# K's first set stored in two halves, warm-up matmuls ahead of it, the second set before head 0

## The chip, the cores and the metric

The kernel runs on one core of one Trainium2 chip. The metric is the device time of one launch in microseconds, median of three runs: 210.45 us before the change (210.29 to 210.97). The engines of the core are TensorE (PE, with its weight loads as PEld), VectorE (DVE), ScalarE (ACT), GpSimd (POOL) and SyncE (SP), which only issues transfers. They run their own programs and meet by semaphores.

## The reference

x has shape (128, 32, 512): batch, head, time. Stage one is a long convolution with a kernel K that is computed from small parameters, plus D times the input, masked by a length per batch; stage two is a linear layer with bias and a low-rank adapter chosen per batch row. Both add to x.

```
dtA = A * dt[:, None]                       # A = -exp(log_A_real) + 1j * A_imag
Ct  = Cc * (exp(dtA) - 1) / A
K   = 2 * einsum('hn,hnl->hl', Ct, exp(dtA[:, :, None] * arange(L))).real
y   = irfft(rfft(u, 2L) * rfft(K, 2L))[..., :L] + u * D[:, None]
x   = x + y * (arange(L) < length)
x   = x + (x @ base_weight.T + base_bias + (x @ A[id].T) @ B[id].T)
```

## The kernel before

**K.** The lag l is written as 32 a + c, so that exp(dtA l) is a product of two factors and K of one head is a small matrix product, 16 x 32, over 128 rows (64 states, real and imaginary part). VectorE makes dt, the angles and their fraction of a turn, ScalarE the magnitudes (one Exp per head, L504), the sines (L468) and th, POOL the division's parts (`sm`, `mm`, `rc`, `ez`; L353 to L376), and VectorE joins them into the coefficients `ct` (`coefficients`, L659 to L664). The heads are done in four sets of 8 (`GROUPS`). For a set VectorE runs `turns`, `phases`, `whole`, `fraction` (L684 to L698), then ScalarE the sine, then VectorE `multiply` and `scale` (L706 to L713), which write the factors `gg` and `ee`. TensorE's `group(k)` multiplies them into a PSUM bank `k_ps` (L913) and adds D to lag 0 by one more product with a unit row (L915).

**The store of K.** `group_store(k)` on ScalarE rounds the PSUM rows to the short float format (`k_hi`, L479), copies them to `k_sb` (L482), waits for VectorE's `k_low(k)`, the remainder (L670), and issues the store to the DRAM buffer `k_pad` on ScalarE's own DMA queue (L487). High and low parts lie beside each other.

**The convolution.** Head h's Toeplitz matrix is read from `k_pad` as a `strip` of 128 rows, each shifted by one lag (L263, 512 KB with both parts, six buffers). The input of a head, `z_all`, comes by pairs of heads (L240, 512 KB; eight pairs first, the others in between by the table `X_AT`). ScalarE rounds it into `xp` (L462), VectorE takes the remainder (L741). `head(h)` on TensorE does 12 matmuls per head into `z_ps` (L932), and VectorE writes the masked result over `z_all` (L747). A strip is issued when the head six before it is done. Set 0 and set 1 of K are made before head 0, sets 2 and 3 by TensorE after heads 7 and 14 (`K_AFTER`; their vector work is spread by `STEPS_AT`).

**The order on SP.** One program order sets all large transfers: parameters, eight x pairs, then, once set 0 of K is in DRAM (wait at L272), strips 0 to 31 with the later x pairs, the adapter tables A and B and the weights W in halves between them (`X_AT`, `A_AT`, `B_AT`, `W_AT`), x_tile 0 and 1, the two parts of the B table, the bias, x_tile 2 and 3 (L266), and then one tile in and one out per step.

**Warm-up.** `keep_warm(n)` issues n matmuls of 512 columns whose result is not used (L904): 15 between the products of sets 0 and 1, and 2 before head 0.

**Stage two.** 32 tiles of 128 rows: `x1_of` adds the convolution to x (L792), ScalarE rounds (L558), `x1_remainder` follows (L796), `tile_h` multiplies by the gathered A (L959), `h_masked` (L802 to L806), `h_rounded` (L570) and `h_remainder` (L811) prepare h, ScalarE and POOL gather the next A (L550, L412), `tile_base` is the weight product (L971), `tile_b` adds B (L997, L998).

## Time and profile before

| what | us |
|---|---|
| median of 3 runs | 210.45 |
| the profiled execution, its time | 210.57 |
| its span on the core | 208.5 |
| head 0 begins | 21.5 |
| stage two begins (first weight matmul) | 87.07 |
| TensorE busy | 190.8 (91%) |
| VectorE busy | 168.1 (81%) |

The span is what the instructions cover; about 2 us of the launch lie around it. The page divides the span into 40 slices and gives a digit of busy share for each, and the chain of work that ended last is followed back from the last instruction. Line numbers are those of the kernel before.

### The profile page before, as it was taken

Reading aid. Unit: us, or ns where it says so; the run is one execution under the profiler, and the core shown is the slowest. Engines: PE = TensorE matmul, PEld = TensorE weight load, DVE = VectorE, ACT = ScalarE, POOL = GpSimd, SP = SyncE. Lnnn points to the kernel's source line nnn. Section 1 sums busy time; section 2 is a strip of 40 time slices with the busy share of each in tenths; the row PEclk is TensorE's granted clock in tenths of the full one; section 3 lists DMA queues with packets and bytes.
Section 4 is the critical chain, followed back from the end, with each engine's and each line's share of the span. In section 5 each row is a group of like instructions: output and inputs, shape, how many; then the busy total and the mean of one; then the engine's idle time right before and its main releaser. Section 6 shows DMA issues by size and latency. Waiting matters only on the chain.

```text
span 208.5 us, 4394 instructions
## 1 busy us (share of the span) xinstructions
PE 190.8 (91%) x1063; PEld 166.4 (80%) x1063; DVE 168.1 (81%) x368; ACT 120.9 (58%) x354; POOL 90.3 (43%) x144
## 2 busy tenths in 40 slices
PE   0049999999999999899999999999999999999994
PEld 0037999999999899787888888888888888888883
DVE  3985598789799976877999978788888878888662
ACT  2798974343736446237767656657566565656530
POOL 4850000001356778085564645546455464545500
PEclk9999999999999999999999999999999999999999
DMA  5973999999999999983767666677776676765324
GB/s 141 400 310 105 377 410 409 409 413 406 412 411 407 409 407 422 339 262 105 257 238 247 217 207 228 214 201 224 213 222 204 216 229 201 218 200 186 103 101 151
DMA packets 21520, 56.46 MB, mean 271 GB/s; under 512 B 3266, under 2 KB 3970, under 8 KB 21250
## 3 DMA queue, kind: packets, MB, share of 16 engines
q1 hardware_dynamic: 18002, 47.55, 62.2%
q0 software_dynamic: 2560, 8.39, 13.3%
q10 hardware_dynamic: 944, 0.36, 0.7%
q8 instruction: 5, 0.08, 0.2%
q14 instruction: 9, 0.07, 0.1%
HBM read 45.64 MB, written 10.65 MB: 270 GB/s over the span
## 4 chain that ended last, share of the span: by engine, by line
PE 87%; DMA 6%; DVE 4%; POOL 1%; issue 1%; DVEq 0%
PE z_ps L932 26%; PE y_ps L971 20%; PE k_ps L971 20%; PE z_ps L959 7%; DMA strip<-k_pad 5%; PE y_ps L904 3%; PE y_ps L998 2%; PE y_ps L997 2%; PE k_ps L998 2%; PE k_ps L997 2%; PE k_ps L913 1%; DMA par<-params 1%; PE y_ps L1020 1%; PE k_ps L1020 1%; PE y_ps L981 1%
## 5 line engine op out<-in xcount | busy, mean ns | idle before, releaser
L932 PE MATMUL z_ps<-xp,strip 128*128 128x512 f32 (+3 forms) x384 | 63.4, 326 | 0.3 <-DMA strip<-k_pad 0.3
L932 PEld LDWEIGHTS z_ps<-xp,strip 128*128 128x128 f32 x384 | 59.3, 196 | 4.3 <-DMA strip<-k_pad 0.4
L417 POOL DMA_INDIRECT b_hl<-b_tab,b_idx x32 | 37.7, 1178 | 15.3 <-issue 8.5
L412 POOL CAST ag<-a_hl 128x128 fp32r x64 | 23.3, 367 | 41.0 <-PE z_ps L959 30.4
L971 PE MATMUL y_ps<-w_hi,xp 128*128 128x512 f32 x120 | 39.5, 390 | 0.0
L971 PE MATMUL k_ps<-w_hi,xp 128*128 128x512 f32 x120 | 39.5, 390 | 0.0
L550 ACT ACTIVATE ag<-a_hl 128x64 fp32r x128 | 25.6, 249 | 20.5 <-issue 20.3
L462 ACT ACTIVATE xp<-z_all 128x512 fp32r<-128x512 f32 x32 | 19.7, 627 | 19.7 <-PE z_ps L932 18.2
L741 DVE TENSOR_TENSOR xp<-z_all,xp 128x512 fp32r<-128x512 f32 x32 | 26.5, 827 | 5.3 <-ACT xp L462 5.2
L971 PEld LDWEIGHTS y_ps<-w_hi,xp 128*128 128x128 f32 x120 | 22.5, 188 | 4.3
L971 PEld LDWEIGHTS k_ps<-w_hi,xp 128*128 128x128 f32 x120 | 22.5, 188 | 4.2
L747 DVE TENSOR_TENSOR z_all<-z_ps,mask 128x512 f32<-128x512 f32 (+2 forms) x33 | 22.1, 669 | 4.2 <-PE z_ps L932 3.9
L570 ACT ACTIVATE h_hi<-h_m 64x128 fp32r<-64x128 f32 x64 | 19.5, 305 | 9.1 <-DVE h_m L806 7.0
L971 PE MATMUL y_ps<-w_lo,xp 128*128 128x512 f32 x60 | 23.4, 390 | 0.0
L971 PE MATMUL k_ps<-w_lo,xp 128*128 128x512 f32 x60 | 23.4, 390 | 0.0
L399 POOL TENSOR_TENSOR a_hl<-a_raw,a_hl 128x512 fp32r<-128x512 f32 x4 | 6.0, 1512 | 38.5 <-ACT a_hl L540 38.5
L558 ACT ACTIVATE xp<-x_t 128x512 fp32r<-128x512 f32 x30 | 19.0, 632 | 5.5 <-DVE x_t L792 4.8
L959 PEld LDWEIGHTS z_ps<-xp,ag 128*128 128x128 f32 x128 | 19.3, 188 | 3.4 <-issue 0.5
L792 DVE TENSOR_TENSOR x_t<-x_t,z_all 128x512 f32<-128x512 f32 x30 | 20.5, 684 | 0.6 <-DMA x_t<-x_tile 0.6
L796 DVE TENSOR_TENSOR xp<-x_t,xp 128x512 fp32r<-128x512 f32 x30 | 20.3, 677 | 0.7 <-ACT xp L558 0.7
L959 PE MATMUL z_ps<-xp,ag 128*128 128x256 f32 x128 | 20.2, 281 | 0.1
L563 ACT ACTIVATE h_b<-z_ps 64x256 f32<-64x256 f32 x32 | 12.1, 379 | 12.4 <-PE z_ps L959 12.4
(138 smaller groups left out, 239.4 us busy)
## 6 DMA issues: line engine op xcount, KB each, us to landing
strip<-k_pad SPq DMA_DIRECT2D x31, 512.0 KB, 7.9
z_all<-x_conv SPq DMA_DIRECT2D x16, 512.0 KB, 8.5
x_t<-x_tile SPq DMA_DIRECT2D x32, 256.0 KB, 2.8
out<-a_raw SPq DMA_DIRECT2D x31, 256.0 KB, 2.4
a_raw<-a_t SPq DMA_DIRECT2D x2, 512.0 KB, 8.3
x_t<-b_rows SPq DMA_DIRECT2D x2, 512.0 KB, 8.8
w_sb<-w_t SPq DMA_DIRECT2D x2, 512.0 KB, 10.0
b_tab<-b_hl SPq DMA_DIRECT2D x1, 1024.0 KB, 10.1
```

The lines of the kernel that those rows point to most:

```text
L412: last = g.tensor_copy(ag[:, s, :, :, q, :].rearrange("p c e r -> p e c r"), src)
L417: g.indirect_dma_start(out=b_hl[:, t % BS, :].bitcast(F32), out_offset=None, in_=b_tab, in_offset=bass.IndirectOffsetOnAxis(ap=b_idx[:, t: ...
L462: act.activation(xp[:, h % XS, :, 0, :], z_all[:, h, :, :], ACT.Copy).then_inc(xc_hi_done, 1)
L550: last = act.activation(ag[:, s, :, e, q, :], src[:, e, :, :], ACT.Copy)
L570: act.activation(h_hi[o:o + BR, b, :], h_m[:, b, :], ACT.Copy).then_inc(hhi_done, 1)
L741: V.tensor_tensor(xp[:, h % XS, :, 1, :], z_all[:, h, :, :], xp[:, h % XS, :, 0, :].bitcast(F32), ALU.subtract).then_inc(xc_lo_done, 1)
L747: V.tensor_tensor(z_all[:, h, :, b0:b1], in_chunks(z_ps[:, h % ZS, :])[:, :, b0:b1], mask[:, :, b0:b1], ALU.mult).then_inc(z_masked, 1)
L792: V.tensor_tensor(xt, xt, z_rows(t), ALU.add).then_inc(x1_done, 1)
L796: V.tensor_tensor(xp[:, s % XS, :, 1, :], in_chunks(x_t[:, s % XT, :]), xp[:, s % XS, :, 0, :].bitcast(F32), ALU.subtract).then_inc(xlo_do ...
L932: last = nc.tensor.matmul(z_ps[:, h % ZS, m * P:L], strip[:, h % SS, m * P:(m + 1) * P, t], xp[:, h % XS, 0:LC - m, e, :], start=(n == 0), ...
L959: last = nc.tensor.matmul(h_ps[:, s % TS, 0:2 * P], ag[:, s % TS, c, :, :, :].rearrange("p e b r -> p (e b r)"), xp[:, s % XS, c, :, :].re ...
L971: last = nc.tensor.matmul(y_bank(s), xp[:, s % XS, c, e, :], w[:, c, :], start=(n == 0), stop=False)
```

## The change

- `GROUPS` becomes five: set 0 is multiplied, rounded and stored as two groups of four heads, and `SETS` keeps the four sets of 8 for the sines. The two PSUM banks and buffers are used in turn (`KS` = 2), each with its own semaphore `k_stored[s]`.
- ScalarE rounds straight into `k_sb` (`rounded_rows`), so that the second copy is gone. It does so after 3, 2 and 3 of the second set's magnitudes.
- The first three stores are issued by SP (`store_k`), the first two before and after the last of the eight x pairs, the third at h = 6. The last two are issued by ScalarE as before.
- Strip 1 is loaded in halves as strip 0.
- TensorE issues 12 warm-up matmuls as soon as POOL has set a buffer to one, 5, 4, 4 and 5 after four events of the preparation, then groups 0 and 1, then 10, 3 and 5 more, and the product of the second set, all before head 0.
- For the sets 2 and 3 the D matmul is replaced by an addition by VectorE in PSUM (`k_first_lag`).
- On POOL the unit matrix is built later, two operations of `mm` come before the reciprocal's result, and two scalings go to ScalarE (L516 and L517 of the changed kernel). The factor 2 is in the table.
- One x pair and one half of W come one head later in SP's order.

```
-GROUPS = ((0, 8), (8, 16), (16, 24), (24, 32))
+SETS = ((0, 8), (8, 16), (16, 24), (24, 32))
+GROUPS = ((0, 4), (4, 8), (8, 16), (16, 24), (24, 32))
-X_AT = {7: 8, 10: 9, 13: 10, 15: 11, 18: 12, 20: 13, 22: 14, 24: 15}
+X_AT = {7: 8, 10: 9, 13: 10, 15: 11, 18: 12, 20: 13, 22: 14, 25: 15}
-A_AT, B_AT, W_AT = {9: 0, 12: 1}, {17: 0, 19: 1}, {24: 0, 26: 1}
+A_AT, B_AT, W_AT = {9: 0, 12: 1}, {17: 0, 19: 1}, {24: 0, 27: 1}
-K_AFTER = {2: 7, 3: 14}
-WARM_0, WARM_1 = 15, 2
+K_AFTER = {3: 7, 4: 14}
+WARM = (12, 5, 4, 4, 5)
+WARM_K = (10, 3, 5)
...
-            for n in range(2, PRE):
+            for n in range(2, PRE - 1):
                 load_pair(n)
+            for k in range(KS):
+                sp.wait_ge(k_lo_done, k + 1)
+                store_k(sp, k)
+                if k == 0:
+                    load_pair(PRE - 1)
...
+                if h == SS:
+                    sp.wait_ge(k_lo_done, BY_SP)
+                    store_k(sp, BY_SP - 1)
                 if h >= SS:
                     sp.wait_ge(conv_done, h + 1 - SS)
-                if h == 0:
-                    load_strip(h, 0, 0, L // 2, strip_begun)
-                    load_strip(h, 0, L // 2, L, strip_landed[0])
+                if h < 2:
+                    load_strip(h, h, 0, L // 2, strip_begun[h])
+                    load_strip(h, h, L // 2, L, strip_landed[h])
...
             g.memset(zero[:, :], 0.0).then_inc(zeroed, 1)
+            pool.wait_ge(zeroed, 1)
+            g.memset(xp[:, XS - 1, :, 0, :].bitcast(F32), 1.0).then_inc(warm_ready, 1)
...
+            link(g.tensor_tensor(mm[:, 1, 1, :], sm[:, 6, :], sm[:, 4, :], ALU.subtract))
+            link(g.tensor_tensor(mm[:, 1, 0, :], sm[:, 5, :], sm[:, 7, :], ALU.add))
             pool.wait_ge(th_ready, 1)
...
             g.tensor_tensor(ez[:, :], th_1[:, :], rr[:, 1, :], ALU.mult).then_inc(ez_ready, 1)
-            link(g.tensor_tensor(mm[:, 1, 1, :], sm[:, 6, :], sm[:, 4, :], ALU.subtract))
-            link(g.tensor_tensor(mm[:, 1, 0, :], sm[:, 5, :], sm[:, 7, :], ALU.add))
...
-            magnitudes(*GROUPS[1])
-            group_store(0)
-            group_sines(1)
+            magnitudes(8, 11)
+            rounded_rows(0)
+            magnitudes(11, 13)
+            rounded_rows(1)
+            magnitudes(13, 16)
+            set_sines(1)
             split_x(1)
-            magnitudes(16, 18)
-            group_store(1)
+            magnitudes(16, 17)
+            rounded_rows(2)
+            magnitudes(17, 19)
             split_x(2)
-            magnitudes(18, 24)
+            magnitudes(19, 24)
+            act.wait_ge(warmed, 1)
             split_x(3)
...
+            def k_first_lag(k):
+                (h0, h1), s = GROUPS[k], k % KS
+                dve.wait_ge(k_done, k + 1)
+                lag_0 = k_ps[0:1, s, 0:(h1 - h0) * NC:NC]
+                V.tensor_tensor(lag_0, lag_0, d_sb[:, h0:h1], ALU.add).then_inc(d_added, 1)
```

TensorE's program up to the first strip matmuls of head 0, before the change:

```order
L913 MATMUL k_ps<-ee,gg 16x32 [waits factors,zeroed,d_in]
L913 MATMUL k_ps<-ee,gg 16x32 x7
L915 MATMUL k_ps<-d_sb,row 16x8
L904 MATMUL y_ps<-xp 128x512 [waits xc_hi_done]
L904 MATMUL y_ps<-xp 128x512 x14
L913 MATMUL k_ps<-ee,gg 16x32 [waits factors]
L913 MATMUL k_ps<-ee,gg 16x32 x7
L915 MATMUL k_ps<-d_sb,row 16x8
L904 MATMUL y_ps<-xp 128x512 x2
L932 MATMUL z_ps<-xp,strip 128x512 [waits xc_lo_done,strip_begun]
```

And the same place of the changed kernel, from the warm-ups (L951) that wait for the angle on:

```order
L951 MATMUL y_ps<-xp 128x512 [waits sines_ready]
L951 MATMUL y_ps<-xp 128x512 x4
L962 MATMUL k_ps<-ee,gg 16x32 [waits factors,zeroed,d_in]
L962 MATMUL k_ps<-ee,gg 16x32 x3
...
L951 MATMUL y_ps<-xp 128x512 x10
L951 MATMUL y_ps<-xp 128x512 [waits reduced]
L951 MATMUL y_ps<-xp 128x512 x2
L951 MATMUL y_ps<-xp 128x512 [waits sines_ready]
L951 MATMUL y_ps<-xp 128x512 x4
L962 MATMUL k_ps<-ee,gg 16x32 [waits k_lo_done,factors]
L962 MATMUL k_ps<-ee,gg 16x32 x7
L967 MATMUL k_ps<-d_sb,row 16x8
```

Eighteen warm-ups now stand between `turn_ready` and the first product, where none stood, and the product of the second set comes directly before head 0.

SP's issues from the x pairs to strip 8, before the change:

```order
L240 DMA z_all<-x_conv 128x1024 x6
L263 DMA strip<-k_pad 128x512 [waits k_stored,pad_stored]
L263 DMA strip<-k_pad 128x512
L263 DMA strip<-k_pad 128x1024 x5
L283 DMA ids<-ids_all 128x160
L263 DMA strip<-k_pad 128x1024 [waits conv_done] x2
L240 DMA z_all<-x_conv 128x1024
L263 DMA strip<-k_pad 128x1024 [waits conv_done,k_stored]
```

And in the changed kernel:

```order
L250 DMA z_all<-x_conv 128x1024 x5
L230 DMA k_pad<-k_sb 16x4x64 [waits k_lo_done]
L250 DMA z_all<-x_conv 128x1024
L230 DMA k_pad<-k_sb 16x4x64 [waits k_lo_done]
L279 DMA strip<-k_pad 128x512 [waits k_stored0,pad_stored]
L279 DMA strip<-k_pad 128x512 x3
L279 DMA strip<-k_pad 128x1024 x2
L279 DMA strip<-k_pad 128x1024 [waits k_stored1]
L279 DMA strip<-k_pad 128x1024
L302 DMA ids<-ids_all 128x160
L230 DMA k_pad<-k_sb 16x8x64 [waits k_lo_done]
L279 DMA strip<-k_pad 128x1024 [waits conv_done] x2
```

Three stores of K have moved into SP's queue, two of them ahead of the first strip with one x pair between them, and the third behind strip 5 and the ids.

## Rows read from the trace of the kernel before

**Rows 1.** The page: DMA share in 40 slices, and the chain by engine.
```profile
DMA  5973999999999999983767666677776676765324
...
PE 87%; DMA 6%; DVE 4%; POOL 1%; issue 1%; DVEq 0%
```

**Rows 2.** The chain of waits to 60 us: start, duration, what.
```profile
13.44 1.01 PE k_ps L913 x16
14.45 0.15 PE k_ps L915 x2
...
21.51 15.60 PE z_ps L932 x96
```

**Rows 3.** Timeline of ACT from 10 to 16 us: start, duration, engine, line, operation.
```profile
10.25 0.63 ACT L468 ACTIVATE work<-work 128x512 f32<-128x512 f32 x1 [0.31 <-DVE work L698]
...
12.71 1.91 ACT L504 ACTIVATE mag<-tab,zr 128x48 f32<-128x48 f32 x8
14.64 0.37 ACT L479 ACTIVATE k_hi<-k_ps 16x256 fp32r<-16x256 f32 x1
...
15.65 0.33 ACTq L487 DMA_DIRECT2D k_pad<-k_sb  x1
```

**Rows 4.** Timeline of DVE from 7 to 16 us.
```profile
7.32 0.18 DVE L650 TENSOR_SCALAR cs_x<-an 128x32 f32<-128x32 f32 x1
...
11.29 0.29 DVE L662 TENSOR_TENSOR cs_m<-cs,mm 128x128 f32<-128x128 f32 x1 [0.60 <-POOL mm L376]
...
11.88 0.42 DVE L706 TENSOR_TENSOR work<-work,ct 128x256 f32<-128x256 f32 x1
...
15.14 0.41 DVE L670 TENSOR_TENSOR k_sb<-k_ps,k_hi 16x256 f32<-16x256 f32 x1
15.48 0.67 DVE L698 TENSOR_TENSOR work<-work 128x512 f32<-128x512 f32 x1
```

**Rows 5.** Timeline of POOL.
```profile
10.73 0.46 POOL L376 TENSOR_TENSOR mm<-mm,rr 128x128 f32<-128x128 f32 x1
13.43 0.57 POOL L380 IOTA mask<- 128x512 int32 x1 [2.25 <-DVE ee L713]
```

**Rows 6.** SP's timeline; issues with size and median time to landing (14:18, then 30:70).
```profile
17.42 3.38 SPq L263 DMA_DIRECT2D strip<-k_pad  x7
...
27.53 2.09 SPq L263 DMA_DIRECT2D strip<-k_pad  x2
...
strip<-k_pad SPq DMA_DIRECT2D x2, 256.0 KB, 3.4
...
k_pad<-k_sb ACTq DMA_DIRECT2D x2, 32.0 KB, 5.6
```

**Rows 7.** Stretches: length; busy per engine (instructions); PEclk, DMA share, GB/s.
```profile
14.00:15.40 1.40, 1.40 (x13) 1.19 (x11) 1.33 (x4) 1.34 (x5) 1.26 (x4) 1.00 0.21 85
...
17.42:19.50 2.08, 2.08 (x8) 1.64 (x7) 1.47 (x5) 2.06 (x3) 0.00 (x0) 1.00 0.36 95
19.50:21.00 1.50, 1.50 (x22) 1.02 (x21) 0.47 (x1) 0.92 (x4) 0.00 (x0) 1.00 0.74 250
...
30.00:80.00 50.00, 49.70 (x332) 46.46 (x331) 44.18 (x74) 24.70 (x44) 19.08 (x19) 1.00 1.03 409
```

**Rows 8.** Timeline of PE from 52 to 90 us.
```profile
72.38 13.91 PE L932 MATMUL z_ps<-xp,strip 128*128 128x512 f32 x84 [0.30 <-DMA strip<-k_pad]
87.07 1.16 PE L981 MATMUL y_ps<-w_hi,xp 128*128 128x512 f32 x4 [0.78 <-DVE xp L870]
```

**Rows 9.** Start of stage two: timeline of DVE, and the chain.
```profile
89.09 0.69 DVE L792 TENSOR_TENSOR x_t<-x_t,z_all 128x512 f32<-128x512 f32 x1 [0.57 <-DMA x_t<-x_tile]
...
94.25 0.11 issue
```

**Rows 10.** Stretches with the matmuls of L904 alone: length, PE and PEld, PEclk, DMA.
```profile
14.50:18.20 3.70, 3.67 (x9) 2.90 (x10) 1.00 0.08 13
18.20:20.10 1.90, 1.90 (x8) 1.24 (x6) 1.00 0.57 160
```

More of the change, by code:

```diff
@@ L698, in fraction, with group @@
                     V.tensor_tensor(x, u, v, ALU.subtract).then_inc(reduced, 1)
+                return [turns, phases, whole, fraction]
+            def group(k):
+                (h0, h1), s = GROUPS[k], k % KS
+                n, of = h1 - h0, h0 // G
+                i0, i1 = h0 % G, h0 % G + h1 - h0
                 def multiply():
-                    dve.wait_ge(sines_ready, k + 1)
+                    dve.wait_ge(sines_ready, of + 1)
                     if k >= KS:
@@ L750, in _ @@
             small_angles()
-            turns, phases, whole, fraction, multiply, scale = group(0)
+            turns, phases, whole, fraction = set_of(0)
             turns()
@@ L758, in _ @@
             coefficients()
-            multiply()
-            scale()
-            turns, phases, whole, fraction, multiply, scale = group(1)
+            for k in range(KS):
+                multiply, scale = group(k)
+                multiply()
+                scale()
+            turns, phases, whole, fraction = set_of(1)
+            k_low(0)
             turns()
+            k_low(1)
             phases()
             whole()
-            k_low(0)
             fraction()
+            multiply, scale = group(KS)
             remainder(0)
@@ L770, in _ @@
             remainder(1)
-            k_low(1)
+            k_low(KS)
             masks()
@@ L774, in _ @@
             remainder(3)
-            beside = {h: do for k, at in STEPS_AT.items() for h, do in zip(at, group(k))}
+            beside = {h: do for k, at in STEPS_AT.items() for h, do in zip(at, set_of(k) + group(k + 1))}
             for h in range(XS, NH):
@@ L934, in head @@
                 last.then_inc(conv_done, 1)
+            pe.wait_ge(warm_ready, 1)
+            keep_warm(WARM[0])
+            for n, (ready, count) in enumerate(((turn_ready, 1), (angle_ready, 1), (cs_ready, 1), (sines_ready, 1))):
+                pe.wait_ge(ready, count)
+                keep_warm(WARM[1 + n])
             pe.wait_ge(d_in, 16)
```

129 lines of the change are left out of this document (71 added, 58 removed).

## The prediction

> **What bounds the kernel now.** I read the page first: TensorE holds 87% of the chain that ended last [rows 1]. That looks like a kernel where only TensorE counts. The DMA row of the same page says otherwise: its digit is 9 from the fifth slice to the seventeenth, about 21 to 88 us, so I took the stretches. From 30 to 80 us the 16 DMA engines are fully busy at 409 GB/s [rows 7]. Both run full side by side, and the chain shows only the one that ends last.
>
> Who ends last is read where they meet. In the convolution TensorE needs 15.60 us for 8 heads, 1.95 each [rows 2], and is stopped once for a strip, by 0.30 us, ten heads after the last product, at head 25 [rows 8]. At the start of stage two VectorE waits 0.57 us for a DMA, x_tile number 2, before it can add it (L792) at 89.09 [rows 9]. Everything behind is a fixed sequence: ScalarE rounds the tile, VectorE takes the remainder and the masked h (L802 to L806), ScalarE rounds h and gathers A, and TensorE goes on with tile_h(2) at 94.36, after 0.11 us that the chain puts down to no work at all [rows 9]. From there the chain never leaves TensorE for long. So the end is set by the landing of x_tile 2, the last of a ring of transfers that SP issues in order and that has run full since the first strips. TensorE's own path is less than 0.6 us better than it. The question is therefore how much earlier the strip stream starts, not how much earlier head 0 does.
>
> The stream starts with the first store of K: SP is idle from its eighth x load until 17.42, when it issues the first strip [rows 6]; the store was issued by ScalarE at 15.65 and took 1.7 us [rows 3, 6].
>
> **First store, step by step.** Before: set 0's product ends at 14.60, ScalarE rounds at 14.64 behind eight magnitudes (1.91 us from 12.71, 0.24 each) and copies, VectorE subtracts from 15.14 to 15.55, the store goes out at 15.65, and the strip 1.77 us later [rows 2 to 4].
> - POOL: the last subtraction and sum of mm go ahead of the reciprocal, so the scaling (10.73, 0.46) can follow ez directly. VectorE's wait of 0.60 at L662 goes, and L706 starts at 11.3 instead of 11.88 [rows 4, 5]. Late next is ct itself, since the sine is done at 10.88 [rows 3].
> - The four operations of set 0 (11.88 until TensorE starts at 13.44, 1.56 us) on half the elements: about 1.1, by the fixed part in rows such as 0.29 for 128 elements against 0.42 for 256 [rows 2, 4]. Group 0's factors at 12.4, its 8 small matmuls and D by 13.2 at the latest (1.01 us for 16 before), group 1's by 14.1.
> - ScalarE: three magnitudes instead of eight: 12.71 + 0.72 = 13.43. That is later than 13.2, so ScalarE's order decides, with 0.2 us to spare. Rounding 128 instead of 256 elements: 0.30 (0.37 before), the second copy is gone; the subtraction about 0.30 (0.41). 13.43 + 0.30 + 0.30 = 14.03, issue 14.13, first strip 14.13 + 1.77 = 15.90.
> - That is **1.52 us** earlier than 17.42. The store now goes through SP's queue behind seven x pairs; the eight were all but in at 14.00 (85 GB/s over the next 1.40 us is 0.12 MB, a quarter of a pair [rows 7]), so the seven are in well before 14.1: no wait. Store 1 is issued about 14.9, behind pair 7, whose 1.28 us (0.52 MB at 409 GB/s) fall into a time in which DMA had next to nothing (17.42 to 19.50: 95 GB/s, and before it less) [rows 7].
>
> **What the stream makes of it.** From the first issue to 21.00 the DMA moved 2.08 x 95 + 1.5 x 250 = 0.57 MB in 3.58 us; at 409 it would be 1.46 MB [rows 7]. So the start costs 2.2 us of full rate; I put 1.0 of it down to the way from the issue to the first packet (an estimate: in 2.08 us only 0.5 us worth of full rate moved) and 1.2 to a slow beginning. No row shows the start with half strips for head 1 and with pair 7 and a store just ahead. Bounds: strip 1, now in halves too, goes at 250 instead of 409 GB/s: 0.52 MB cost 2.1 instead of 1.28, +0.8 us; or pair 7 keeps the engines running and the slow 1.2 us vanish, -1.2. I take +0.15, nearer to no change, since the same two halves open the stream and nothing else in it grows. Sum: 1.52 - 0.15 = **1.37 us**.
>
> The rest of the ring has the same bytes in the same order up to two swaps of x and W loads, which change who is late inside the convolution, not when x_tile 2 lands. The third store goes through SP's queue behind strips 2 to 5 and the ids. Before, on ScalarE's queue, a store took 5.6 us in the full stretch [rows 6]; now it lands with the ids, about 28, and strip 8 waits for it, where it was issued at 27.53 [rows 6]. Strips 6 and 7 and a pair are queued by then, 3 x 1.28 = 3.8 us of work, more than the 3.4 us that a half strip takes from its issue into an idle DMA [rows 6]: I cost it at nothing. If that cover is short, its price is the missing part, up to 1 us. The Trainium skill (DMA: Bandwidth & Descriptors, Queues, rings and completion order) says that an engine consumes one ring's descriptors in order and takes turns between rings. By that rule the store in SP's ring lands behind strip 5 and store 1 behind pair 7, as reckoned above from the order of issue, where a ring of its own would have let them pass; the 5.6 us that a store took on ScalarE's ring beside a full SP ring show that even there it does not pass quickly.
>
> **Edits that should not reach the end.** TensorE: before head 0 stands set 1's product. VectorE's phases for it start about 0.8 later, once the first subtraction is done at 14.0: fraction ready near 16.9 (it ended at 16.15 before), sine to 17.5 with its 0.63, factors at 18.95 (set 0's took 1.4 to 1.5), product 0.70, head 0 at 19.8 instead of 21.51: 1.7 us [rows 2, 4]. The 30 + 18 warm-up matmuls lie in waiting time if they run at 0.23 us each: five from 17.5 end at 18.7, before the factors. The swaps bring strip 25 one transfer (1.28 us) forward, which covers its 0.30 wait; two D products (0.15 each [rows 2]) leave TensorE, and VectorE's additions of one row take their place beside it. TensorE is so 1.7 + 0.3 + 0.3 = 2.3 us earlier at the end of the convolution, and VectorE reaches L792 by that much earlier: it then waits 0.57 + 2.3 - 1.37 = 1.5 us for x_tile 2. About 0.9 us of TensorE's gain is thus given back.
>
> The profiled execution took 210.57 with a span of 208.5, the median of the three runs is 210.45. 210.57 - 1.37 = **209.2**.
>
> **Rivals.**
> - The stream's start comes more than 2.3 earlier in effect (1.52 + the 1.2 of the bound), or x_tile 2 is not what ends last: then TensorE's 2.3 us decide, **208.2**. For it: pair 7 is in flight when strips arrive. Against: the 0.57 wait of rows 9 is plain.
> - The gain is eaten in the stream: halves at 250 GB/s (+0.8) and pair 7 with store 1 in front (0.3, my guess for what its own start costs), so 1.52 - 1.1 = 0.42: **210.1**. For it: half strips are the only ones seen at 250. Against: they are also the first of the stream.
> - Warm-up at the lower clock, slower. Before, 9 warm-up matmuls filled 3.70 us (0.41 each) and then 8 took 1.90 (0.24), both under a granted clock of 1.00: the first pace is 1.2 GHz, the second 2.4 [rows 10]. In the new program 18 stand between turn_ready (7.50 by L650 [rows 4]) and group 0. At 0.23 they end near 12.1, in time. If TensorE is still or again at 1.2 GHz after its pause before turn_ready they cost 18 x 0.43 = 7.7 us: group 0 at 15.3, product 16.05, store 16.8, first strip 18.55, 1.1 later than before: **211.7**. It begins to cost when group 0 starts after 12.7 (0.75 before ScalarE's 13.43), and the sign turns when it starts after 14.0. Against it: TensorE has twelve others ahead of these, from about 1.8 on (a memset of POOL comes first, as wide as the iota of 0.57 [rows 5]), so work from 1.8 to about 6.2, and before, the faster pace came 3.7 us after the first. The Trainium skill (TensorE: Matmul & The Clock Gate, HAM oscillation — how this bites in real kernels) says that idle stretches bring the lower clock back. By that rule the pause here, 6.2 to 7.5, is the danger; in this trace the pause of 0.78 us at L981 is followed by 4 matmuls in 1.16 us, the fast pace [rows 8], so up to there the trace does not show it.
> - The change does not do what it says (first store no earlier): ScalarE's table load to 12.70 stays fixed, and three instead of eight magnitudes are certain, so I give it nothing of its own.
>
> **Chances.** Forecast 0.62, its own range 208.6 to 209.8. TensorE decides 0.18. Gain eaten 0.12. Slower 0.08. 0.3% (0.63 us) is about what a measurement of this kernel can't tell from no change. Faster: 0.62 + 0.18 plus a small part of the third, 0.81; same 0.11; slower 0.08. The range reaches from a little below the first rival to just past the second: 208.0 to 210.2; the slow case is left out.
>
> **What would show it.** First store issued on SP near 14.1, first strip near 15.9. Head 0 near 19.8. VectorE's idle time before the addition of x_tile 2 (now L792) grows from 0.57 to about 1.5 us, with the landing of x_tile 2 near 87.6, and TensorE waits before L997 or tile_h(2) by about 0.9 us more. Strip 25 no longer stops TensorE. Warm-up matmuls at 0.23 us from turn_ready on; at 0.43 the third rival holds. I am wrong if the idle time before that addition is gone, if DMA shows a hole between 28 and 32 us (strip 8), or if the DMA share between strips and 20.5 us is far from 250 GB/s.

## The result, and the profile after

The changed kernel took **211.89 us** in the median of five runs (211.01 to 212.05); the 210.45 us of the kernel before is likewise a median of five. The ratio is 1.0043, with a 95% interval of [1.0028 to 1.0058]: a little slower, where 209.2 was forecast. On another occasion, beside three of its relatives, it took 211.47 (12 runs, 210.44 to 212.41; ratio 1.0036 [1.0016 to 1.0056]). The profiled execution took 211.50 with a span of 209.8.

The page of the changed kernel: DMA share and GB/s in 40 slices of 5.2 us, and the chain by engine.

```profile
DMA  5959999999999999965778776767666677764334
GB/s 140 397 217 273 380 391 277 416 417 407 406 412 412 406 409 414 364 216 154 235 232 248 223 218 207 236 193 219 200 229 214 203 225 213 223 205 176 109 100 152
...
PE 77%; DMA 11%; DVE 4%; issue 3%; ACT 2%; SPq 1%; ACTq 0%; DVEq 0%
```

The share row reads as before [rows 1]: full from the start of the strips. The row below shows what it hides: the seventh slice, 31 to 37 us, moves 277 GB/s between neighbours of 391 and 416. The engines are "busy" there with packets that take longer: a busy share says that packets are under way, not how fast they move. DMA's part of the chain rose from 6 to 11%, PE's fell from 87 to 77% [rows 1].

**The start came as forecast.** The chain of waits of the changed kernel, first and middle part (start, duration, what):

```profile
13.55 0.28 ACT k_sb L500
13.85 0.29 DVE k_sb L702
14.16 1.46 DMA k_pad<-k_sb
...
17.96 8.82 DMA strip<-k_pad
26.79 0.04 issue
26.83 10.00 PE z_ps L984 x60
...
63.93 10.42 DMA strip<-k_pad
```

And PE's timeline, rows that answer to [rows 2, 8, 10]:

```profile
1.66 5.49 PE L951 MATMUL y_ps<-xp 128*128 128x512 f32 x12 [1.66 <-POOL xp L358]
7.58 1.42 PE L951 MATMUL y_ps<-xp 128*128 128x512 f32 x5 [0.44 <-DVE cs_x L675]
9.19 3.28 PE L951 MATMUL y_ps<-xp 128*128 128x512 f32 x13 [0.19 <-POOL cs_x L390]
12.64 0.39 PE L962 MATMUL k_ps<-ee,gg 128*16 128x32 f32 x8 [0.16 <-DVE ee L754]
...
19.84 6.34 PE L984 MATMUL z_ps<-xp,strip 128*128 128x512 f32 x36
26.83 0.51 PE L984 MATMUL z_ps<-xp,strip 128*128 128x512 f32 x1 [0.64 <-DMA strip<-k_pad]
...
64.16 9.99 PE L984 MATMUL z_ps<-xp,strip 128*128 128x512 f32 x60 [0.25 <-DMA strip<-k_pad]
74.40 11.95 PE L984 MATMUL z_ps<-xp,strip 128*128 128x512 f32 x72 [0.25 <-DMA strip<-k_pad]
87.06 1.16 PE L1041 MATMUL y_ps<-w_hi,xp 128*128 128x512 f32 x4 [0.71 <-DVE xp L917]
...
95.05 0.47 PE L1057 MATMUL y_ps<-b_hl,h_hi 128*128 128x512 f32 x1 [1.28 <-DVE h_lo L858]
```

Twelve warm-ups take 0.46 us each in the mean (the slow pace), then 18 take 0.26: the fast pace is there from `turn_ready` on, and group 0 starts at 12.64. Head 0 begins at 19.84 instead of 21.51. Yet the first weight matmul comes at 87.06, before at 87.07 [rows 8]: waits for strips (0.64, 0.25, 0.25 and smaller ones of heads 0 to 2) took back all 1.7 us. At the start of stage two VectorE waits longer than before for x_tile 2 (before 0.57, until 89.09 [rows 9]). It comes to this place no earlier, at 90.51 - 1.94 = 88.57 us against 88.52 before; only the transfer is later:

```profile
90.51 0.69 DVE L839 TENSOR_TENSOR x_t<-x_t,z_all 128x512 f32<-128x512 f32 x1 [1.94 <-DMA x_t<-x_tile]
```

**Where the stream lost its lead.** SP's timeline, to be held against [rows 6]:

```profile
14.16 0.34 SPq L230 DMA_DIRECT2D k_pad<-k_sb  x1
14.54 0.43 SPq L250 DMA_DIRECT2D z_all<-x_conv  x1
15.02 0.43 SPq L230 DMA_DIRECT2D k_pad<-k_sb  x1
15.70 4.04 SPq L279 DMA_DIRECT2D strip<-k_pad  x8
19.78 0.48 SPq L302 DMA_DIRECT2D ids<-ids_all  x1
20.82 0.32 SPq L230 DMA_DIRECT2D k_pad<-k_sb  x1
...
29.82 0.81 SPq L279 DMA_DIRECT2D strip<-k_pad  x2
```

The issues of 18 to 30 us (size, median us to landing) have for the third store:

```profile
k_pad<-k_sb SPq DMA_DIRECT2D x1, 32.0 KB, 9.0
```

and SP's waits (total, times, longest):

```profile
SPq L279 <- DMA k_pad<-k_sb: 5.1, 2, 3.6
```

The first strip is issued at 15.70, 1.72 us earlier than before. The third store, issued at 20.82, lands 9.0 us later; 3.6 us of SP's waiting are for it, and strip 8 behind it goes out at 29.82, 2.3 us later than before. The stretches (columns as in [rows 7]):

```profile
17.42:19.50 2.08, 1.91 (x19) 1.25 (x18) 2.01 (x6) 2.05 (x4) 0.84 (x2) 1.00 1.06 312
19.50:21.00 1.50, 1.50 (x18) 1.31 (x14) 0.81 (x3) 1.18 (x5) 0.00 (x0) 1.00 0.94 238
...
31.00:37.00 6.00, 6.00 (x44) 5.58 (x44) 5.34 (x12) 2.44 (x5) 0.00 (x0) 1.00 0.99 283
37.00:80.00 43.00, 42.46 (x279) 39.47 (x276) 37.17 (x61) 20.12 (x36) 19.29 (x19) 1.00 1.03 411
```

Every transfer is spread over 16 DMA engines, so the trace records 16 landings of each; below is the last of them, in us from the span's start.

| transfer | before | after | earlier by |
|---|---|---|---|
| strip 0, first half | 20.47 | 19.33 | 1.14 |
| strip 2 | 24.32 | 23.96 | 0.36 |
| strip 3 | 25.66 | 26.77 | -1.11 |
| pair 8 | 33.89 | 33.40 | 0.49 |
| A, first half | 37.73 | 38.30 | -0.57 |
| strip 24 | 68.50 | 69.22 | -0.72 |
| x_tile 1 | 82.56 | 84.11 | -1.55 |
| x_tile 2 | 88.97 | 90.38 | -1.41 |

Of the 1.72 us, 1.36 are gone by strip 2, 0.13 come back by pair 8, 1.06 go while strip 8, strip 9 and the half of A pass, 0.15 on the long way to strip 24, 0.69 at the end (the lag is still 0.71 at strip 31, then 1.55 at x_tile 1). In sum 3.26 were lost and 0.13 won back, which turns a lead of 1.72 into a lag of 1.41.

At strip 3 a second quantity shows: the last of the 16 landings came 2.80 us after the first (before 0.31). Fifteen of them lie within 1.24 us, the last one comes 1.56 behind these, and so it stays up to pair 8. The third store shows it too: issued at 20.82, it had 15 of its 16 landings by 28.2 and the last at 29.8. SP waits for all 16, so a single late landing held strip 8 back by 1.6 us. Before, on ScalarE's queue, the 16 landings of this store lay between 27.00 and 27.52.

Where the late landing comes from is not shown. In time it goes with an instruction fetch, a packet of 16 KB that took 0.92 us from 24.35 on, while strip 3 was landing. Other late landings do so as well: a fetch of 1.08 us from 81.86 on runs while x_tile 1 lands, and in the kernel before one of 0.97 us from 28.79 on runs while strip 5 lands, whose last landing came 0.91 us behind the other fifteen. Further fetches left the spread as it was, and the trace does not say which DMA engine a packet used.

### The profile page after: what moved, and what is told of

It is laid out like the page before. It is cut to its first block, busy times and chain, and to the rows that moved or that the text cites. A ratio compares the mean times of both kernels' runs of the same rounds, so it can differ in the third digit from the quotient of the medians.

```text
span 209.8 us, 4461 instructions
## 1 busy us (share of the span) xinstructions
PE 200.1 (95%) x1092; PEld 171.9 (82%) x1092; DVE 169.8 (81%) x375; ACT 120.0 (57%) x353; POOL 92.1 (44%) x143
## 4 chain that ended last, share of the span: by engine, by line
PE 77%; DMA 11%; DVE 4%; issue 3%; ACT 2%; SPq 1%; ACTq 0%; DVEq 0%
PE z_ps L984 23%; PE k_ps L1031 20%; PE y_ps L1031 18%; DMA strip<-k_pad 9%; PE z_ps L1019 7%; PE y_ps L1057 2%; PE y_ps L1058 2%; PE k_ps L1058 2%; PE k_ps L1057 2%; DMA par<-params 1%; SPq L279 1%; DMA k_pad<-k_sb 1%; PE y_ps L1080 1%; PE k_ps L1080 1%; ACT L524 1%
## 5 line engine op out<-in xcount | busy, mean ns | idle before, releaser
L984 PE MATMUL z_ps<-xp,strip 128*128 128x512 f32 (+3 forms) x384 | 64.2, 326 | 1.3 <-DMA strip<-k_pad 1.1
L484 ACT ACTIVATE xp<-z_all 128x512 fp32r<-128x512 f32 x32 | 19.8, 627 | 21.3 <-PE z_ps L984 19.4
L839 DVE TENSOR_TENSOR x_t<-x_t,z_all 128x512 f32<-128x512 f32 x30 | 20.5, 685 | 1.9 <-DMA x_t<-x_tile 1.9
```

What stands on the lines that cost most here:

```text
L484: act.activation(xp[:, h % XS, :, 0, :], z_all[:, h, :, :], ACT.Copy).then_inc(xc_hi_done, 1)
L839: V.tensor_tensor(xt, xt, z_rows(t), ALU.add).then_inc(x1_done, 1)
L984: last = nc.tensor.matmul(z_ps[:, h % ZS, m * P:L], strip[:, h % SS, m * P:(m + 1) * P, t], xp[:, h % XS, 0:LC - m, e, :], start=(n == 0), ...
```

## The experiments

The first eight asked what undoing edits gives, singly and together, and whether x_tile 2 sets the end; the next four what the changed kernel and the third store are worth by themselves; the last six why the ring slows down. The numbers behind each time are its ratio to the kernel before, measured on the same occasion, and the 95% interval. The time before was 210.61 to 210.77 in the median of each occasion. Ratios are the fairer comparison between occasions: some kernels spread over 2 us, and their medians then differ more than their ratios. Landings and waits are those of one profiled execution of each kernel.

**Strip 1 whole again** (`a1_strip1_whole`), at SP and at TensorE:
```
-                if h < 2:
+                if h < 1:
```


> The changed kernel with strip 1 in one piece again. Theory (half strips are slow pieces of the stream): strip 2 lands at about 23.0 instead of 23.96, the stream stays 0.8 to 1.0 us ahead, x_tile 2 lands near 89.5 instead of 90.38, time 210.9 to 211.1. Rival (the stream's first three us are slow whatever the pieces are): strip 2 lands at 23.9, time 211.8 as the changed kernel.


210.96 us (210.11 to 211.89), 1.0013 [0.9994 to 1.0032]. The time is the one that the theory gave, but not by its mechanism: strip 2 landed at 24.26 (theory 23.0, with halves 23.96). In this trace the size of the first pieces is not what makes the start slow. What did go earlier is strip 8, issued at 28.69 (29.82 in the changed kernel).

**Third store by ScalarE** (`a2_store3_act`):
```
-                if h == SS:
-                    sp.wait_ge(k_lo_done, BY_SP)
-                    store_k(sp, BY_SP - 1)
...
             rounded_rows(2)
             magnitudes(17, 19)
...
+            act.wait_ge(k_lo_done, 3)
+            store_k(act, 2)
```


> The changed kernel with the third store of K (the second set) issued by ScalarE on its own queue, as before the change. Theory (strip 8 waits for a store that stands behind strips 2 to 5 and the ids in SP's ring, so that the ring runs empty and starts slowly again): strip 8 is issued at about 27 instead of 29.80, A's first half lands near 37.2 instead of 38.30, the 31 to 37 us stretch runs at over 400 GB/s instead of 240 to 300, time 210.8. Rival (that stretch is slow for another cause, instruction reads or the pieces' order): the rate there stays under 330 GB/s, time 211.8.


210.70 us (210.23 to 212.71), 1.0011 [0.9988 to 1.0033]. The time came as the theory said, the rate did not: strip 8 went out at 28.22 (29.82 in the changed kernel, theory 27), and 31 to 37 us ran at 335 GB/s, near the rival's 330. The store had 15 of its 16 landings by 27.10 here, the last at 28.22.

**Both** (`a3_both`):

> Both edits: strip 1 in one piece and the third store by ScalarE. Theory: the two losses add, x_tile 2 lands near 88.3, time 209.8 to 210.2. Rival (TensorE's path, which is 1.7 us better at head 0, sets the end as soon as one of the two is gone): the same time as the better of the two alone.


210.86 us (210.01 to 211.62), 1.0006 [0.9989 to 1.0023]. The two edits do not add. In this trace, of an execution of 211.60 us, the last landing of strips 2 to 5 came up to 4.0 us after the first, and TensorE waited 1.03, 0.35 and 0.67 us for strips before 27 us.

**The kernel before with x_tile 2 ahead of the B tables** (`a4_before_xt2_early`):
```
             load_x_tile(1, 1)
+            load_x_tile(2, 2)
             ... the two parts of the B table, the bias
-            load_x_tile(2, 2)
```


> The kernel before, with x_tile 2 loaded ahead of the two parts of the B table instead of behind them and the bias. Theory (the landing of x_tile 2 sets the start of stage two and so the end): it lands near 83.2 instead of 88.97, VectorE's wait of 0.57 us goes, TensorE goes on with tile_h(2) 0.3 to 0.6 us earlier, time 209.9 to 210.2. Rival (TensorE's own path sets it): 210.5, no change. A third way: the B table lands 0.65 us later and its gathers become the limit, time 210.5 to 211.


210.13 us (209.80 to 210.35), 0.9971 [0.9958 to 0.9984]. VectorE's timeline, the row of [rows 9]:
```profile
88.44 0.69 DVE L792 TENSOR_TENSOR x_t<-x_t,z_all 128x512 f32<-128x512 f32 x1
```
The wait is gone and the addition 0.65 us earlier. That x_tile 2 sets the end of the kernel before was right, and its worth is near the bound of the prediction (less than 0.6 us): 0.5 us by the medians, 0.6 by the ratio.

**All x pairs ahead of the stores** (`b1_pairs_first`):
```
-            for n in range(2, PRE - 1):
+            for n in range(2, PRE):
                 load_pair(n)
...
-                if k == 0:
-                    load_pair(PRE - 1)
```


> The changed kernel with all eight x pairs issued ahead of the stores, as before the change, so that nothing large stands between the first store and the strips. Theory (pair 7 and store 1 keep the ring moving while the strips are issued, and one of the 16 engines falls behind there: spread of a strip's 16 landings 1.2 to 2.8 us by strip 3, where it was 0.3 to 0.6 before): the first store lands at about 16.0 behind pair 7, first strip issued 16.1, spread at strip 3 under 1.0, strip 3 lands near 25.0, time 210.4 to 210.9. Rival (halves and instruction reads make the lag, pair 7 nothing): spread at strip 3 over 2, time 211.8 to 212.2, since the first strip is also issued 0.4 later.


210.78 us (210.10 to 211.75), 0.9997 [0.9981 to 1.0014]. The time is as in the theory; the spread at strip 3, 1.93 us, lies between the theory (under 1.0) and the rival (over 2).

**x_tile 2 early in the changed kernel** (`b2_after_xt2_early`), the edit of `a4`:

> The changed kernel with x_tile 2 loaded ahead of the B table's two parts. Theory (in the changed kernel VectorE waits 1.94 us for x_tile 2, and that is the whole loss at the end, since the first weight matmul is at 87.06 as before): that wait goes, tile_h(2) starts near 94.3 instead of 95.7, time 210.2 to 210.6. Rival (another wait of stage two, the gathers of B behind a late table, takes its place at once): 211.3 or more.


210.94 us (210.12 to 211.99), 1.0009 [0.9991 to 1.0028]: VectorE's wait is gone (L839 at 89.47), but strips stop TensorE until 24.59, 27.20, 62.39, 64.95 and 75.19, and the first weight matmul comes at 87.86. So in the changed kernel the wait for x_tile 2 is a part of the loss and not all of it.

**Strip 1 whole, third store by ScalarE, x_tile 2 early** (`b3_whole_act_xt2`) (the edits of `a3` and `a4` together):

> Strip 1 in one piece, the third store by ScalarE and x_tile 2 early. Theory: stage two is no longer tied to x_tile 2 and the time follows the end of the convolution, which the slowest DMA engine sets (spread over 2 us in the run with both edits): 210.0 to 210.5 and wide from run to run. Rival (the first two edits carry gains once x_tile 2 is out of the way): under 209.6.


210.05 us (209.40 to 211.17), 0.9975 [0.9959 to 0.9991], as the theory said.

**These with all pairs first** (`b4_all`):

> The same three edits and all x pairs ahead of the stores. Theory (with the ring at rest when the strips begin, the slowest engine's lag stays under 1 us and the 1.4 us that the first store is earlier reach the end of the convolution): first weight matmul near 85.8, time 208.9 to 209.4. Rival (the lag comes whatever stands before the strips): 210.0 to 210.5 as the run without this edit.


209.71 us (209.51 to 210.51), 0.9957 [0.9938 to 0.9975]: faster than both kernels, but slower than the theory (208.9 to 209.4); the first weight matmul comes at 86.66, not near 85.8. Its DVE timeline:
```profile
59.65 1.32 DVE L760 CAST id_f<-ids 128x160 f32<-128x160 int32 x1
61.00 0.25 DVE L761 TENSOR_SCALAR id_f<-id_f 128x160 f32<-128x160 f32 x1
```
and its PE timeline, with a new wait:
```profile
64.22 21.72 PE L981 MATMUL z_ps<-xp,strip 128*128 128x512 f32 x132 [1.38 <-DVE xp L779]
```
VectorE's id operations (head 20) stand ahead of the remainders for which TensorE waits before head 21.

**The changed kernel again** (`c1_after_again`):

> The changed kernel unchanged, beside before, on the chip of the three kernels sent with it. Its 211.89 came from five runs of its own call, while its four relatives with one edit each gave 210.7 to 211.0, near before's 210.6. If it is really slower than they are (their edits then gained about 1 us each): 211.5 to 211.9. If the five runs were a draw from a wide spread (its relatives' runs go from 210.1 to 212.0): median 210.9 to 211.3. If it repeats near 210.5, the change is worth nothing either way and my loss terms are noise.


211.47 us, between the two cases; its interval says slower than before, so the loss is real. The relatives with one edit each (`a1`, `a2`, `b1`, `b2`) lie 0.5 to 0.8 below it by their medians; their intervals overlap with this one, so what each edit is worth is not well known.

**The id operations spread** over heads 17, 19, 21 and 23 (`c2_ids_spread`, on `b4_all`; `adapter_ids` is cut in four parts):
```
-                if h == 20:
-                    adapter_ids()
+                if h in (17, 19, 21, 23):
+                    adapter_ids((17, 19, 21, 23).index(h))
```


> The version with all four edits (strip 1 whole, third store by ScalarE, x_tile 2 ahead of the B tables, all x pairs ahead of the stores), and in addition VectorE's seven id operations, which all stood at head 20 (2.6 us in a row), spread over heads 17, 19, 21 and 23. Theory: in that version TensorE waited 1.38 us at head 22 for VectorE's remainder behind the id operations; the wait goes or falls under 0.3, and with TensorE's path now the one that ends last, most of it is gained: 208.5 to 209.1. Rival A: x_tile 2 or the B tables are late again, so the wait only moves: 209.5 to 209.8. Rival B: the id operations cost the same wherever they stand, because each step of VectorE there is as full as at head 20: several waits of 0.3 to 0.6, 209.7.


209.73 us (209.69 to 209.77), 0.9958 [0.9945 to 0.9971]. The theory is out. TensorE still waits 1.37 us in one piece, now before head 20. Two of the moved operations fell beside GpSimd's additions and took 1.33 and 1.29 us, where at head 20 only the cast had (1.32). The several short waits of rival B were not seen.

**Three edits without the early x_tile 2** (`c3_without_xt2`):

> The version with three edits: strip 1 whole, third store by ScalarE, all x pairs ahead of the stores; x_tile 2 in its old place behind the B tables. With x_tile 2 ahead as well it was 209.71. Theory: x_tile 2 decides the end, so without that swap 0.3 to 0.6 us are lost: 210.0 to 210.3, with VectorE waiting 0.5 to 1.0 us before the addition of x_tile 2. Rival: the three edits of the stream's start bring x_tile 2 in early enough by themselves and TensorE's 1.4 us wait decides: 209.7, no wait of VectorE there.


210.15 us (209.78 to 210.71), 0.9980 [0.9969 to 0.9991], with a wait of 0.41 us for x_tile 2. The time is as in the theory, the wait a little under it.

**The third store's step alone, in the kernel before** (`c4_before_store1_sp`; there it is the second store):
```
+                if h == SS:
+                    sp.wait_ge(k_hi_put, 2)
+                    sp.wait_ge(k_lo_done, 2)
+                    sp.dma_start(k_pad[...], k_sb[...]).then_inc(k_stored, 16)
```
and the same store is taken out of ScalarE's program.


> The kernel before with one step of the change alone: the store of the second set goes out on SP's queue at h = 6, behind strips 2 to 5 and the ids, instead of on ScalarE's. Theory: it lands about 9 us after its issue (5.7 before), strip 8 is issued 1.5 to 2.3 us later than 27.54, the stretch from 31 to 37 us falls from 414 to about 300 GB/s, and x_tile 2 lands up to 1.1 us later: 211.0 to 211.7, VectorE's wait before it 1.2 to 1.7 us (0.57 before). Rival, as I reckoned in the prediction: it lands about 28, what is queued covers it, cost nothing: 210.4 to 210.7, stretch above 400 GB/s.


**212.31 us** (210.83 to 214.02), 1.0062 [1.0036 to 1.0087]. This one step, costed at nothing in the prediction, costs 1.3 us by the ratio [0.8 to 1.8] and 1.7 by the medians; the runs spread over 3 us. The theory (at most 1.1) was too low. The rows below are of an execution of 213.25 us, one of the slower ones. In it no single landing of the store stands out (the first came at 28.23, 15 were in by 29.61, the last at 30.12): here the place in the ring alone makes it late. The issue of the store in this kernel:
```profile
k_pad<-k_sb SPq DMA_DIRECT2D x1, 32.0 KB, 8.9
```
its stretch, where the share too is below one:
```profile
31.00:37.00 6.00, 6.00 (x40) 5.65 (x38) 5.34 (x12) 2.81 (x5) 0.00 (x0) 1.00 0.91 273
```
and VectorE's row at x_tile 2:
```profile
92.05 0.69 DVE L801 TENSOR_TENSOR x_t<-x_t,z_all 128x512 f32<-128x512 f32 x1 [1.27 <-DMA x_t<-x_tile]
```

**One transfer more in the queue** (`d1_longer_queue`, the changed kernel with one entry moved):
```
-A_AT, B_AT, W_AT = {9: 0, 12: 1}, ...
+A_AT, B_AT, W_AT = {7: 0, 12: 1}, ...
```


> The changed kernel with one transfer moved: the first half of the adapter table A (512 KB) goes out at h = 7, ahead of strip 8's wait for the third store, instead of at h = 9. The same bytes, but 1.28 us more of them are queued while SP waits. Theory: what the third store costs is that the ring runs short before strip 8 is issued (3.6 us were left) and then runs slow; with 4.9 us left the stretch from 31 to 37 us rises from 283 to over 380 GB/s, x_tile 2 lands 0.7 to 1.1 us earlier, and the time falls to 210.5 to 210.9 (211.5 for the changed kernel in two calls). Rival: the slow stretch belongs to the store or to what is read then (strips from rows just written), not to the length of the queue: stretch below 320 GB/s, 211.3 to 211.7.


**210.08 us** (209.65 to 211.28), 0.9986 [0.9971 to 1.0000], faster than the theory said. The store is where it was, issued at 20.85, and the bytes are the same; it landed at 29.03 (29.79 in the changed kernel's first trace, 29.49 in its second). SP's timeline:
```profile
25.31 0.44 SPq L255 DMA_DIRECT2D a_raw<-a_t  x1
29.04 2.22 SPq L279 DMA_DIRECT2D strip<-k_pad  x3
```
and the stretch:
```profile
31.00:37.00 6.00, 6.00 (x46) 5.58 (x46) 5.31 (x12) 2.42 (x4) 0.00 (x0) 1.00 1.02 410
```
283 GB/s became 410, and time came back: 1.1 us by the ratios (1.0036 and 0.9986), 1.4 by the medians. Since the store landed 0.5 to 0.8 us earlier in this trace, a fairer pair is the second trace of the changed kernel (`c1`) and the one with this entry and one more moved (`f1`, below). There the stores landed at 29.49 and 29.43, and up to 37 us only the queue differs:
```profile
31.00:37.00 6.00, 6.00 (x52) 5.58 (x51) 5.31 (x11) 2.38 (x4) 0.00 (x0) 1.00 1.00 306
31.00:37.00 6.00, 6.00 (x40) 5.65 (x38) 5.31 (x11) 2.83 (x5) 0.00 (x0) 1.00 1.03 410
```
The first row is `c1`, the second `f1`. The rate behind the wait follows the length of the queue at the wait, not the store as such.

**The same at strip 16** (`d2_b_before_16`, on `c3`: `B_AT` `{17: 0, ...}` to `{15: 0, ...}`):

> The version with strip 1 whole, third store by ScalarE and all x pairs first (210.15), with one transfer moved: the first half of the B table goes out at h = 15, ahead of strip 16's wait for the fourth store, instead of at h = 17. There strip 16 was issued at 45.68 with 3.0 us left in the ring, and 46 to 50 us ran at 328 GB/s. Theory: that is where its lead of 1.9 us in the stream (strip 10) was given back; with 1.28 us more queued the stretch rises above 390 and x_tile 2 lands 0.5 to 1.0 us earlier (87.7 to 88.2), VectorE no longer waits for it; TensorE's own wait of 1.4 at head 22 then decides: 209.6 to 209.9. Rival: the stream is slow there for another reason, nothing moves: 210.0 to 210.3.


209.77 us (209.40 to 209.81), 0.9959 [0.9947 to 0.9972]. The stretch of 46 to 50 us in `c3`:
```profile
46.00:50.00 4.00, 4.00 (x27) 3.77 (x26) 3.46 (x8) 2.64 (x5) 0.00 (x0) 1.00 1.01 328
```
and here:
```profile
46.00:50.00 4.00, 4.00 (x28) 3.78 (x27) 3.52 (x8) 2.57 (x5) 0.22 (x1) 1.00 1.03 410
```
x_tile 2 landed at 87.74 (88.67 without), and nobody waited for it: the theory held.

**The id operations in VectorE's gaps** (`d3_ids_in_gaps`, on `b4_all`), and **both** (`d4_gaps_and_b`):
```
                         k_low(k)
+                        for part in {3: (0, 1), 4: (2, 3)}[k]:
+                            adapter_ids(part)
...
-                if h == 20:
-                    adapter_ids()
```


> The version with all four edits (209.71), with VectorE's id operations put into two gaps in which it waited 1.1 us for ScalarE (behind the remainders of the third and fourth K group, heads 11 and 18), away from GpSimd's splitting of the tables, beside which each ran at 1.2 to 1.3 us instead of 0.25. Spread over heads 17 to 23 they gained nothing. Theory: VectorE is the bound in heads 16 to 22, and 1.5 to 2.5 us of its work leave that stretch, so TensorE's wait of 1.37 goes or falls under 0.5; the end follows by 0.4 to 1.0: 208.7 to 209.3. Rival: x_tile 2 or the B tables' landing is what ends last behind it: 209.6 to 209.8, with the wait only moved to the start of stage two.


209.70 us (209.50 to 210.23), 0.9962 [0.9948 to 0.9976], as the rival said: the wait of 1.37 is gone, but strips stop TensorE by 0.28 and 0.24 and the gathered B by 0.39. The cast takes 0.22 us in its gap; beside GpSimd's splitting of the tables it took 1.32.

> The edits of both other versions together: all four edits, id operations in VectorE's gaps, and the first half of the B table ahead of strip 16. Theory: TensorE's wait at head 22 gone and the stream 0.5 to 1.0 us further ahead, so neither B tables nor tiles are late at the start of stage two: 208.4 to 209.0, the fastest. Rival: the stream was no longer late once x_tile 2 went first, so it equals the version without the B half moved, within 0.2 us.


**208.21 us** (208.19 to 208.25), **0.9886 [0.9872 to 0.9900]**, better than its forecast of 208.4 to 209.0. The ids in gaps alone moved `b4_all` by nothing, the entry alone moved `c3` by 0.4; together they gain 1.5 over `b4_all`. That each had hidden the other fits the waits (in `d3` the wait for VectorE had given way to waits for strips and the gathered B), but the entry alone in `b4_all` was not run. Its PE timeline has no wait for DMA left, and stage two starts 1.8 us earlier than before [rows 8]:
```profile
85.28 1.16 PE L1043 MATMUL y_ps<-w_hi,xp 128*128 128x512 f32 x4 [0.71 <-DVE xp L919]
```
Its cast, in the gap:
```profile
39.30 0.22 DVE L762 CAST id_f<-ids 128x160 f32<-128x160 int32 x1
```
Its chain by engine, to be held against [rows 1]:
```profile
PE 87%; DVE 7%; ACT 2%; issue 1%; DMA 1%; DVEq 0%; ACTq 0%
```

**What of this works with the stores left on SP.** Both entries moved in the changed kernel (`f1_two_entries`), and these with the early x_tile 2 and the ids in gaps (`f2_all_with_sp_stores`):

> The changed kernel with two entries of SP's table moved and nothing else: the first half of table A at h = 7 instead of 9, the first half of the B table at h = 15 instead of 17. With the first alone it took 210.08, and x_tile 2 still stopped VectorE for 1.53 us at 88.95 while strip 16 had over 3 us queued (46 to 50 us at 399 GB/s). Theory: what is left of the stream's loss lies at its start (strips 0 to 3), so the second entry adds little: 209.8 to 210.1. Rival: the second short queue costs 0.5 us or more here too, as it did in the version with the start undone: 209.4 to 209.7.


209.77 us (209.26 to 211.47), 0.9958 [0.9940 to 0.9976]: between the theory and its rival. The second entry gave 0.3 us by the medians, 0.6 by the ratios.

> The changed kernel with both entries moved, x_tile 2 ahead of the B tables, and the id operations in VectorE's gaps; its three stores through SP, pair 7 between them and strip 1 in halves stay. It differs from the fastest version (208.21) only in the start of the stream and the third store. Theory: the third store costs nothing once the queue behind it is long; the start costs TensorE 0.3 to 0.7 us in strip waits before head 3 and the stream about 1 us: 208.6 to 209.4, strip waits of TensorE below 27 us as in its relatives. Rival: the stores through SP cost as such: 209.5 to 210.


209.71 us, 0.9949 [0.9931 to 0.9967] (eleven runs from 208.86 to 211.00; a twelfth took 684.11 and is left out): slower than the theory, and where the rival put it (209.5 to 210: the stores through SP cost as such). This kernel lies 1.3 us above `d4` by the ratios and 1.5 by the medians, and it varies while `d4` does not, though behind both of its waits the trace shows the full rate (411 and 410 GB/s). It differs in pair 7 between the stores, strip 1's halves, the third store on SP, and the first half of A at h = 7. Which of the four carries the difference was not run. The trace cannot tell either: it is of the fastest execution (208.86), in which strips stopped TensorE only once, for 0.28 us, and the gathered B for 0.15.

## Why the prediction was wrong

**Right: what bounds the kernel before.** x_tile 2 decides its end (`a4`). In the changed kernel it stands last too (VectorE's wait of 1.94), but strips stand close behind: with that wait gone the time fell by only 0.5 us (`b2`).

**Right: the first store, step by step.** Issued at 14.16 (forecast 14.13), first strip at 15.70 (15.90), gain 1.72 (1.52). The product of set 1, head 0 at 19.84 (19.8), the fast pace of the warm-ups and the second short group hold too. The third rival falls: slower was right as a sign, for another reason. Its condition never arose. The prediction let the first twelve warm-ups end at 6.2 and feared a pause until 7.5; at the slow pace they lasted until 7.15, and the pause was 0.43 us. So this run does not test what the longer pause would have done.

**Wrong: "What the stream makes of it", the third store.** The prediction wrote: "Strips 6 and 7 and a pair are queued by then, 3 x 1.28 = 3.8 us of work, more than the 3.4 us that a half strip takes from its issue into an idle DMA [rows 6]: I cost it at nothing." The step that failed is to treat the 16 DMA engines as one. For the one that is last the amount was right: at 29.80 it still had 3.59 us to do. But the store is only done when the last of the 16 has landed its part: 15 were in by 28.2, as forecast ("about 28"), and the last came at 29.79. And the cover ends when the first of them runs out of work: it finished pair 8 at 30.67, 0.87 us after the issue. In x_tile 2's landing 1.06 us were lost here. The bound ("up to 1 us") was too narrow: measured by itself the step costs 1.3 to 1.7 us (`c4`), and 1.1 to 1.4 come back when one more transfer is queued (`d1`). The rule of the Trainium skill (DMA: Bandwidth & Descriptors, Queues, rings and completion order) that the prediction cited agrees with the trace: the store landed at 29.79, strip 5 ahead of it in the same ring at 29.35. Before, on ScalarE's ring, the same set's store was issued behind strip 5 as well, at 21.79, and it landed at 27.52, ahead of strip 5 (first landing at 27.99, last at 29.31). The prediction read from its 5.6 us that "even there it does not pass quickly"; it did pass.

Over all 20 kernels the same quantity orders the rate. It is taken at the moment when SP issues strip 8, or strip 16, after waiting for a store: how long until the engine that is first through has finished what was queued, by the first of the 16 landings of the last transfer in the queue. Beside it stand the GB/s of 31 to 37 us (strip 8) or 46 to 50 us (strip 16). The table has 18 of the 40 cases.

| left on the first engine, us | cases | GB/s behind it |
|---|---|---|
| 0.75, 0.87, 1.39 | b2, after, c1 | 280, 283, 306 |
| 1.18, 1.27, 1.31 (strip 16) | c2, c3, d3 | 334, 328, 327 |
| 1.72, 1.75, 1.90 | c4, b1, a3 | 273, 316, 339 |
| 2.20, 2.36 | a1, a2 | 356, 335 |
| 2.55 (strip 16), 2.77, 3.31 | d1, f1, d1 | 399, 410, 410 |
| 3.11, 3.14, 3.34, 4.54 | c3, b4, d4, before | 408, 412, 408, 414 |

In all 40 cases the rate is 399 or more where 2.5 us or more are left, and in 14 of the 15 below that it is 364 or less (the fifteenth, `a2` at strip 16, has 2.27 left and runs at 404). By the last engine the order is not so clean: `a2` has 5.97 us left there and runs at 335. This is an order over single traces; only `d1`, `d2` and `f1` changed the queue on purpose. It fits the gains of `a1`, `a2` and `b1`, each of which let strip 8 go out 1.1 to 1.6 us earlier. Why the rate stays low for some 6 us, at a full share, is not settled; the runs show it and no more.

**Wrong: "What the stream makes of it", the start (+0.15).** The lead is down by 1.36 us at strip 2, where 0.15 was reckoned. The bound of +0.8 was too small, and its cause was not the half strips (`a1`). From 19.50 to 21.00, with the strips earlier, the DMA moved 238 GB/s (before 250 [rows 7]), though pair 7 had kept it busy until just before (its last landing came at 18.2). `f2` against `d4` puts 1.3 to 1.5 us on the start, the third store's place and one entry for A together. What makes the start slow stays open.

**Wrong: "the rest of the ring has the same bytes in the same order".** A stream that runs ahead meets the next wait with a shorter queue. In `c3` strip 10 landed 1.93 us earlier than before, strip 21 1.09 and strip 22 only 0.17. The first loss lies behind strip 16, which waits for the fourth store, whose time TensorE sets; the second is one late landing of the 16 (0.95 us behind the other fifteen, 0.20 at strip 21). With `B_AT` moved (`d2`) strip 22 landed 1.67 us earlier than before and x_tile 2 1.23; without it x_tile 2 led by 0.30. So in that kernel 1.37 us would not have reached x_tile 2. In the changed kernel itself this step cost nothing, since strip 16 had 4.60 us left and 410 GB/s behind it. There 0.69 us were lost between strip 31 and x_tile 1 instead, beside the instruction fetch named above; no experiment bears on it.

**The sum.** x_tile 2 was to land near 87.6 and landed at 90.38, 2.8 us later; the time was 2.7 us over the forecast. Of this 1.21 are the start, 1.06 the third store, 0.69 the end and 0.15 the way between; 0.20 and 0.13 came the other way.

**Wrong, and near its number by luck: "TensorE is so 1.7 + 0.3 + 0.3 = 2.3 us earlier at the end of the convolution".** The first weight matmul came at 87.06, 0.01 us earlier than before, because strips stopped TensorE. VectorE's wait did grow from 0.57 to 1.94, near the 1.5 that was to be the sign of a faster TensorE. In truth it grew because x_tile 2 came 1.41 us later.

**The rival that came nearest** was "the gain is eaten in the stream" (210.1, chance 0.12), right in kind and too small by 1.8 us. The prediction's own sign for it, a hole at 28 to 32 us, was named and missed in one point: the share shows no hole (0.98 from 28 to 32 us, 0.99 from 31 to 37), only the GB/s column does (373 and 283).

## What to carry to other kernels

Where an in-order queue waits for a transfer that stands in the same queue, the wait ends with the **last** of the DMA engines, and in these runs the cover was what the **first** of them still had to do, not bytes divided by the full rate. Here 2.5 us of it were enough in every case, and putting one more ready transfer ahead of the wait was worth 1.1 to 1.4 us for one number in a table. Look at GB/s beside the share, since slow packets count as busy. And where undoing single edits gives nothing, look for a second engine just behind the first: two edits that were worth 0 and 0.4 us, each beside another kernel, gave 1.5 together.

## What the runs showed that I had not expected

- The 32 KB store of the second set took 9.0 us in the full ring of SP, where on ScalarE's ring beside it stores took 5.6 [rows 6]. Over the kernels it took 7.8 to 9.3 us on SP's ring and 5.7 to 7.3 on ScalarE's.
- With less than 2.5 us left on the first engine, 31 to 37 us ran at 273 to 356 GB/s with a share of 0.91 to 1.03, against 408 to 414 otherwise.
- The first and the last landing of a transfer drift apart, from 0.31 us (strip 3, before) to 2.80 (after) or 4.0 (`a3`), and under full load the distance can stay: before it was 1.8 us from strip 6 to x_tile 1, while in the changed kernel it fell to 1.78 at strip 8.
- VectorE's cast of 128x160 takes 0.22 us alone and 1.32 beside GpSimd's additions of 128x512; its remainder of 128x512 takes 0.68 or, beside them, mostly 1.2 to 1.8.
